# Attention stage of a gated block: row sums from TensorE to VectorE, W1 applied to the attended rows, norm of x on VectorE, bias on Pool

## The chip, the cores and the metric
One core of a Trainium2 chip runs the whole program. TensorE (PE) multiplies matrices from SBUF into PSUM; VectorE (DVE), ScalarE (ACT) and GpSimd (Pool) work on tiles of up to 128 partitions; SyncE (SP) issues most of the DMAs. The engines run at the same time and wait for one another only at semaphores; each takes its own instructions in the order in which they are written. The metric is the time of one execution in microseconds (us), less is better.

## The reference
x has 4 batches of 1024 rows of 256; the context has 154 rows for each batch. What matters, cut down:

```python
x = x + tanh(g_xattn[0]) * xattn(layernorm(x), ctx, w_sim, b_sim, W_qv, b_qv)
x = x + tanh(g_ffn[0]) * ffn(layernorm(x), w_gate, w_up, w_down)

def xattn(h, c, w_sim, b_sim, W_qv, b_qv):
    Sim = (h @ w1)[:, :, None] + (c @ w2)[:, None, :] + einsum('bid,bjd->bij', h * w3, c) + b_sim
    A = softmax(Sim, axis=2)
    hq = einsum('bij,bjd->bid', A, c)                    # attended
    Batt = softmax(max(Sim, axis=2), axis=1)
    hc = einsum('bi,bid->bd', Batt, h)                   # one row for each batch
    return concatenate([h, hq, h * hq, h * hc]) @ W_qv + b_qv
```

The feed-forward part quantizes activations and weights, with the largest values over whole tensors. W_qv has four blocks of 256 rows; W1 below is the second, which multiplies hq.

## The kernel before, in words
All x stays in SBUF (`xa`). The attention stage takes the rows in 16 pieces n of 256 rows, four to a batch b; s = n % 4. It is a pipeline by hand: one loop over m = 0 to 22, written out anew for each engine, in which step m does another operation for another piece. On PE, step m holds project(m - 7), turn_h(m) (transposes of the normed rows), score(m - 1), turn_a(m - 2) (transposes of the softmax), attend(m - 3) and turn_y(m - 8). In a step with m % 4 = 3 the project comes last ("late"), else first. The semaphores' counts order what the engines hand over; PSUM has one bank for each kind of result (`hT_bank`, `s_bank`, `a_bank`, `y_bank`, `hq_bank`, `m_bank`), and two for project.

A piece goes this way: VectorE takes mean and variance (`stats`, L955 to L962), Pool the power -0.5 (L363), VectorE the shift -mean x rstd (`row_shift`, L969), ScalarE the normed rows h (`norm_x`, L736). PE turns h, ScalarE copies hT (L744), PE scores (L454), VectorE adds the context's bias and takes the minimum (`scored`, L989), ScalarE the exponentials (L752), VectorE the reciprocal (L997), ScalarE scales (L761), PE turns, ScalarE copies aT (L768), PE attends (L474), VectorE multiplies the result in PSUM with hT (prT, L1005). Project (L491 to L499) sums three products into one bank: aT with `cw`, prT with W_qv's third block, hT with `we`. VectorE adds it to x (`residual`, L1013), takes the statistics of the second layer norm (L1017 to L1024), Pool the power (L367), VectorE writes y (L1030) and its maximum (L1057).

`cw` is the context times W1 plus the bias b_qv, once for each batch (`context_w`, L430, and `context_wv`, L978); since a softmax row sums to one, aT with cw gives attended x W1 with the bias. `we` holds W_qv's first block plus its fourth times hc. hc needs the softmax over a whole batch: `batch_max` and `batch_shift` take the extreme over 1024 rows, ScalarE the eight columns of weights eb (`batch_exp`, L801), PE the weighted row sums (`row_sum`, L537: eight matmuls, one for each 128 rows, M = 1), VectorE copies the row (`row_copy`, L1073), PE turns it to columns (`batch_cols`, L545), and `summary` (L1077 to L1083) writes we. For the first batch the eight row sums stand as a block in step 6; for the other three they stand between the matmuls of the project in the steps 10, 14 and 18. we(b) is needed by the late project of step 4b + 7.

Beside this run the preparations of the three feed-forward weights: scales on VectorE in m = 8, 12, 16 (L1097), two halves of `weight_q` on Pool (L380), int16 values on VectorE in m = 11, 15, 19 (L1117), a copy on ScalarE (L805), `weight_n` on Pool (L386).

## Time and profile before

| | |
|---|---|
| time, median of 3 runs | 500.15 us (500.15 to 500.7) |
| the profiled execution | 500.24 us, its span 498.0 us |
| PE busy | 467.1 us, 94% |
| VectorE busy | 347.6 us, 70% |
| ScalarE busy | 278.5 us, 56% |
| Pool busy | 42.8 us, 9% |
| mean granted PE clock | 0.983 |

The span runs from the first to the last instruction of the profile; the rest of the execution's time lies around it. The attention stage ends at about 222 us, where the quantized feed-forward part begins. Busy time of PE counts overlapping matmuls once, with modelled ends.

### The profile page before, as it was taken

How to read it: one execution, taken by the hardware profiler on the slowest of the kernel's cores; microseconds unless marked ns; L12 is line 12 of the kernel's file. 1: busy time of each engine (PE TensorE's matmuls, PEld its weight loads, DVE VectorE, ACT ScalarE, POOL GpSimd, SP SyncE). 2: the span in 40 equal slices, each digit the busy share in tenths (PEclk: the TensorE clock that was granted, in tenths of full speed). 3: DMA queues.
4: the chain of work that ended last, by engine and by line, in shares of the span. 5: the costliest groups of instructions: out<-in, count | busy, mean ns of one | idle time of the engine just before them, and what ended most of it. 6: DMA issues, size and time to landing. Idle time of an engine off the chain costs nothing.

```text
span 498.0 us, 6971 instructions
## 1 busy us (share of the span) xinstructions
PE 467.1 (94%) x2542; PEld 306.2 (61%) x2542; DVE 347.6 (70%) x648; ACT 278.5 (56%) x325; POOL 42.8 (9%) x51
## 2 busy tenths in 40 slices
PE   4899999998999979989999999999949999999997
PEld 3787885987488548754444444444414444588886
DVE  6464683687257754769443558999988888898874
ACT  3795241634151200528334379999977677888760
POOL 1111111242013110210000000000100000000000
PEclk9999999998999998999999999999969999999999
DMA  8920000200020020020000000000000000234432
GB/s 246 327 91 1 0 2 12 74 1 1 0 86 0 1 84 2 0 86 0 0 0 0 0 0 0 0 0 1 1 0 0 0 0 0 85 107 128 144 113 103
DMA packets 20671, 21.11 MB, mean 42 GB/s; under 512 B 826, under 2 KB 20393, under 8 KB 20649
## 3 DMA queue, kind: packets, MB, share of 16 engines
q1 hardware_dynamic: 20628, 20.82, 13.2%
q8 instruction: 13, 0.21, 0.2%
q14 instruction: 10, 0.07, 0.1%
q10 hardware_dynamic: 20, 0.00, 0.0%
HBM read 12.43 MB, written 8.39 MB: 42 GB/s over the span
## 4 chain that ended last, share of the span: by engine, by line
PE 56%; issue 17%; DVE 14%; ACT 10%; POOL 1%; DMA 1%; ACTq 0%; POOLq 0%; DVEq 0%
PE ps L672 11%; PE ps L647 10%; PE ps L652 5%; PE ps L495 4%; PE ps L491 4%; PE ps L474 4%; PE ps L499 4%; ACT ag L863 3%; PE ps L537 3%; ACT hid L870 3%; PE ps L454 3%; DVE hid L1279 2%; ACT gq L858 2%; PE ps L440 1%; PE ps L463 1%
## 5 line engine op out<-in xcount | busy, mean ns | idle before, releaser
L647 PE MATMUL ps<-xh,wuh 128*128 128x512 f16 x192 | 73.9, 385 | 9.3 <-DVE gq L1304 7.4
L647 PE MATMUL ps<-xh,wul 128*128 128x512 f16 x192 | 73.8, 384 | 0.0
L652 PE MATMUL ps<-xl,wuh 128*128 128x512 f16 x192 | 58.0, 384 | 0.0
L1251 DVE TENSOR_REDUCE cols<-hid x12 | 27.4, 2286 | 30.5 <-ACT hid L852 30.5
L852 ACT ACTIVATE hid<-ps 128x2048 f32 x12 | 22.5, 1875 | 34.5 <-PE ps L652 34.5
L647 PEld LDWEIGHTS ps<-xh,wuh 128*128 x192 | 19.0, 99 | 34.7 <-issue 11.2
L672 PE MATMUL ps<-wdh,oh 128*128 128x256 f16 x168 | 37.4, 273 | 0.0
L672 PE MATMUL ps<-wdl,oh 128*128 128x256 f16 x168 | 37.4, 273 | 0.0
L647 PE MATMUL ps<-xh,wgh 128*128 128x512 f16 x96 | 36.4, 379 | 0.7 <-DVE xh L1239 0.7
L647 PE MATMUL ps<-xh,wgl 128*128 128x512 f16 x96 | 36.4, 379 | 0.0
L491 PE MATMUL ps<-cw,aT 77*128 77x256 f32 x128 | 35.5, 392 | 0.9 <-ACT cols L801 0.9
L495 PE MATMUL ps<-wv,prT 128*128 128x256 f32 x128 | 35.9, 396 | 0.0
L744 ACT ACTIVATE hT<-ps 128x512 f32<-128x512 f32 x16 | 9.4, 590 | 46.5 <-PE ps L440 46.5
L499 PE MATMUL ps<-we,hT 128*128 128x256 f32 x128 | 33.5, 384 | 0.0
L652 PEld LDWEIGHTS ps<-xl,wuh 128*128 x192 | 19.0, 99 | 23.3 <-issue 1.1
L647 PEld LDWEIGHTS ps<-xh,wul 128*128 x192 | 19.0, 99 | 22.4 <-issue 1.1
L474 PE MATMUL ps<-aT,cx 77*128 77x256 f32 x128 | 30.5, 381 | 0.0
L1304 DVE TENSOR_TENSOR gq<-gq,ps 128x2048 bf16<-128x2048 int16 x11 | 25.2, 2287 | 6.1 <-ACT au L878 6.1
L1265 DVE TENSOR_REDUCE cols<-ps 128x1 f32<-128x2048 f32 x12 | 27.4, 2286 | 2.7 <-PE ps L652 2.7
L924 ACT ACTIVATE oq<-hid,cols 128x1536 int16 (+1 forms) x15 | 23.6, 1572 | 10.2 <-DVE ol L1349 10.2
L1310 DVE CUSTOM_DVE_ANT_0 hid<-pq,au 128x2048 f32<-128x2048 int16 x12 | 27.4, 2286 | 2.6 <-ACT pq L908 1.9
L495 PEld LDWEIGHTS ps<-wv,prT 128*128 128x128 f32 x128 | 23.8, 194 | 8.3 <-issue 5.2
(199 smaller groups left out, 945.9 us busy)
## 6 DMA issues: line engine op xcount, KB each, us to landing
x_scratch<-xa SPq DMA_DIRECT2D x4, 1024.0 KB, 4.4
xo<-x_scratch SPq DMA_DIRECT2D x16, 256.0 KB, 2.7
out_dram<-xo SPq DMA_DIRECT2D x15, 256.0 KB, 2.2
xa<-in_x SPq DMA_DIRECT2D x3, 1024.0 KB, 12.1
xa<-in_x SPq DMA_DIRECT2D x4, 256.0 KB, 4.7
wv<-in_L_xattn_W_qv SPq DMA_DIRECT2D x1, 1024.0 KB, 8.1
wr<-in_L_ffn_w_gate SPq DMA_DIRECT2D x1, 768.0 KB, 9.6
wr<-in_L_ffn_w_up SPq DMA_DIRECT2D x1, 768.0 KB, 11.0
```

Of the source, the lines that this page charges most:

```text
L474: mm = pe.matmul(hq_bank[:, d * PT:(d + 1) * PT], cx[b][0:JP, k, d * P:(d + 1) * P], aT[0:JP, par, k, q], start=k == 0, stop=k == 1)
L491: pe.matmul(o_, aT[0:JP, par, k, q], cw[0:JP, b % 3, k, :], start=k == 0, stop=False)
L495: pe.matmul(o_, prT[:, par, d, q], wv[:, 2 * KD + d, :], start=False, stop=False)
L499: mm = pe.matmul(o_, hT[:, par, d, q], we[:, par, d, :], start=False, stop=d == KD - 1)
L647: pe.matmul(ps[hf][:, q, :], w_[:, d, ds(k * P, P)], xh[:, d, n], start=d == 0 and w_ is wh, stop=False)
L652: mm = pe.matmul(ps[hf][:, q, :], wh[:, d, ds(k * P, P)], xl[:, d, n], start=False, stop=d == KD - 1)
L672: mm = pe.matmul(down_ps(par)[:, t], o_[:, par, k, q], w_[:, k, :], start=not low and k == 0 and w_ is wdh, stop=low and k == KF - 1)
L924: act.activation(oq[:, par], hid[:, :, ds(c * CD, CD)], ACT.Copy, scale=c_co).then_inc(oqa_rdy, 1)
L1251: dve.tensor_reduce(gmx[:, ds(k * 2 + hf, 1)], unit(hid, k, hf), AX.X, ALU.max, apply_absolute_value=True).then_inc(gm_done, 1)
L1265: dve.tensor_reduce(umx[:, u:u + 1], ps_half(u % 2), AX.X, ALU.max, apply_absolute_value=True).then_inc(half_free[u % 2], 1)
L1304: dve.tensor_tensor(g_.bitcast(BF16), g_, ps_half(hf), ALU.mult).then_inc(half_free[hf], 1)
L1310: dve.tensor_tensor_reduce(hid[:, k, hf * HALF:(hf + 1) * HALF], pq[hf][:], au[:, hf, :], 1.0, 0.0, ALU.mult, ALU.max, omx[:, u:u + 1]).th ...
```

## The change
- **Row sums.** The 32 matmuls go. VectorE forms the sum in place, in h's tile 0: h0 x eb0, then seven times h_t x eb_t + h0, each waiting for the one ahead (`hs_rdy`). Four links stand in s = 2 ahead of the reciprocal, four behind the product prT. Then h's tile 0 holds 128 rows of partial sums, and `batch_cols` sums them over the partitions by matmuls with a column of ones. `batch_cols` and `summary` move from s = 2 to s = 3, just ahead of the late project.
- **W1.** `context_w` and `cw` go. ScalarE copies the attended result from PSUM to `hqT` (behind its scaling), project multiplies hqT by W1, and prT is made from hqT and hT, both in SBUF. aT gets a ring of three.
- **Norm of x.** `row_shift` and ScalarE's norm_x go; VectorE does it in one tensor_scalar for each 128 rows ((x - mean) x rstd), for the piece m + 1, at the head of a step, in s = 3 behind summary.
- **Bias.** Pool adds tanh(g) x b_qv to x (`bias_x`), two pieces in each step with s = 0 or 3, once h of that piece is made; residual waits for it (`xb_rdy`).

The diff, cut to its core; of the two functions `attended`, the added one is ScalarE's.

```diff
+            def bias_x(n):
+                pool.wait_ge(h_rdy, n + 1)
+                if n == 0:
+                    pool.wait_ge(txb_rdy, 1)
+                x_ = xa[:, 2 * n:2 * n + 2, :]
+                pool.tensor_tensor(x_, x_, txb[:].unsqueeze(1).broadcast_to([P, 2, D]), ALU.add).then_inc(xb_rdy, 1)
...
                 if 1 <= m and m + 3 < N:
                     row_std(m + 3)
+                if s in (0, 3) and 4 <= m < N + 4:
+                    for n in range(2):
+                        bias_x(m - 4 + n if s == 0 else m - 5 + n)
...
-            def context_w(b):
...
             def attend(n):
                 pe.wait_ge(aT_rdy, n + 1)
-                ge(pe, pr_rdy, n)
+                ge(pe, hqT_rdy, n)
...
-                    for k in range(2):
-                        pe.matmul(o_, aT[0:JP, par, k, q], cw[0:JP, b % 3, k, :], start=k == 0, stop=False)
-                        if summed is not None:
-                            row_sum(summed, 4 * t + k)
+                    for d in range(KD):
+                        pe.matmul(o_, hqT[:, par, d, q], wv[:, KD + d, :], start=d == 0, stop=False)
                     for d in range(KD):
                         pe.matmul(o_, prT[:, par, d, q], wv[:, 2 * KD + d, :], start=False, stop=False)
-                        if summed is not None:
-                            row_sum(summed, 4 * t + 2 + d)
...
-            def row_sum(b, t):
-                mm = pe.matmul(m_bank[0:1, P:P + D], eb[:, t:t + 1], h[:, b % 2, t, :], start=(t == 0), stop=(t == TB - 1))
...
             def batch_cols(b):
-                pe.wait_ge(hrow_rdy, b + 1)
+                pe.wait_ge(hs_rdy, TB * (b + 1))
                 for d in range(KD):
-                    pe.matmul(m_bank[:, HC + d:HC + d + 1], hrow[0:1, d * P:(d + 1) * P], ones[0:1, 0:1], start=True, stop=True)
+                    pe.matmul(m_bank[:, HC + d:HC + d + 1], h[:, b % 2, 0, d * P:(d + 1) * P], ones[:, 0:1], start=True, stop=True)
...
+            def attended(n):
+                act.wait_ge(hq_ps, n + 1)
+                ge(act, f_ps, n - 2 * NP + 1)
+                act.activation(hqT[:, par, :, s * PT:(s + 1) * PT], hq_bank.rearrange("p (d n) -> p d n", d=KD),
+                               ACT.Copy).then_inc(hqT_rdy, 1)
...
+            def norm_x(n):
+                dve.wait_ge(rstd_rdy, n + 1)
+                ge(dve, hc_ps, b - 1)
+                for t in range(2 * s, 2 * s + 2):
+                    i_ = dve.tensor_scalar(h[:, par, t, :], xa[:, b * TB + t, :], mv[:, par, t, 0:1], rstd[:, c:c + 1],
+                                           ALU.subtract, ALU.mult)
...
             def attended(n):
-                dve.wait_ge(hq_ps, n + 1)
+                dve.wait_ge(hqT_rdy, n + 1)
...
+            def row_sum(b, tiles):
+                dve.wait_ge(eb_rdy, b + 1)
+                for t in tiles:
+                    ge(dve, hs_rdy, TB * b + t)
+                    if t == 0:
+                        i_ = dve.tensor_scalar(h[:, par, 0, :], h[:, par, 0, :], eb[:, 0:1], None, ALU.mult)
+                    else:
+                        i_ = dve.scalar_tensor_tensor(h[:, par, 0, :], h[:, par, t, :], eb[:, t:t + 1], h[:, par, 0, :],
+                                                      ALU.mult, ALU.add)
...
+                if s == 2 and 1 <= b <= B:
+                    row_sum(b - 1, range(0, 4))
                 if 1 <= m <= N:
                     normed(m - 1)
                 if 3 <= m <= N + 2:
                     attended(m - 3)
+                if s == 2 and 1 <= b <= B:
+                    row_sum(b - 1, range(4, TB))
+                if s == 3 and 1 <= b <= B:
+                    summary(b - 1)
+                if s == 3 and m + 1 < N:
+                    norm_x(m + 1)
                 if LAG <= m and late:
                     residual(m - LAG)
```

Two places in the engines' orders. First VectorE in step 10 (s = 2), before: the shift of piece 12, summary of the second batch, the unit of the first weight, y, reciprocal, product.

```order
L969 SCALAR_TENSOR_TENSOR cols<-cols 128x2
L1077 RECIPROCAL cols<-ps 128x1
L1079 TENSOR_SCALAR cols<-ps,cols 128x2
L1083 SCALAR_TENSOR_TENSOR we<-wv,cols 128x256 x2
L1107 TENSOR_REDUCE cols<-ps 128x1
L1109 TENSOR_SCALAR cols<-cols 128x1
L1110 RECIPROCAL cols<-cols 128x1
L1111 TENSOR_SCALAR cols<-cols 128x1
L1112 TENSOR_SCALAR wsc<-wsc,cols 128x48
L1030 TENSOR_SCALAR yb<-xa,cols 128x256 x2
L997 RECIPROCAL cols<-cols 128x2
L1005 TENSOR_TENSOR prT<-ps,hT 128x2x256
```

The same step of the changed kernel, from the unit's last instruction on (L1055 and L1057 are row_sum, L981 the product, L1034 the maximum of y).

```order
L1100 TENSOR_SCALAR wsc<-wsc,cols 128x48
L1006 TENSOR_SCALAR yb<-xa,cols 128x256 x2
L1055 TENSOR_SCALAR h<-h,cols 128x256
L1057 SCALAR_TENSOR_TENSOR h<-h,cols 128x256 x3
L973 RECIPROCAL cols<-cols 128x2
L981 TENSOR_TENSOR prT<-hqT,hT 128x2x256
L1057 SCALAR_TENSOR_TENSOR h<-h,cols 128x256 x4
L1034 TENSOR_REDUCE cols<-yb 128x1
```

The chain of eight has come in around reciprocal and product, and summary has left this step. Second, PE in step 11 (s = 3) before: attend, turn_y, context_bias and then the late project.

```order
L474 MATMUL ps<-aT,cx_84 128x256 x4
L510 MATMUL ps<-ident,yb 128x128 x4
L422 MATMUL ps<-cxT,w2b 128x154 x2
L491 MATMUL ps<-cw,aT 128x256 x2
L495 MATMUL ps<-wv,prT 128x256 x2
```

And in the changed kernel (L537 and L538 are batch_cols, L493 the product with W1).

```order
L477 MATMUL ps<-aT,cx_84 128x256 x4
L508 MATMUL ps<-ident,yb 128x128 x4
L435 MATMUL ps<-cxT,w2b 128x154 x2
L537 MATMUL ps<-ones,h 128x1 x2
L538 MATMUL ps<-cols,ones 128x1
L493 MATMUL ps<-wv,hqT 128x256 x2
L495 MATMUL ps<-wv,prT 128x256 x2
```

Batch_cols now stands directly ahead of the project that needs its result through VectorE's summary.

## Rows read from the trace of the kernel before

**Rows 1.** The page: busy us of an engine, share of the span, instructions.

```profile
PE 467.1 (94%) x2542; PEld 306.2 (61%) x2542; DVE 347.6 (70%) x648; ACT 278.5 (56%) x325; POOL 42.8 (9%) x51
```

**Rows 2.** Windows between late projects: length, busy of each engine (instructions), granted clock, DMA.

```profile
48.33:95.30 46.97, 46.97 (x251) 36.75 (x251) 29.42 (x103) 16.79 (x47) 8.04 (x10) 1.00 0.07 23
95.30:146.28 50.98, 48.13 (x243) 37.50 (x243) 31.08 (x96) 18.58 (x51) 10.78 (x10) 0.97 0.06 22
146.28:187.30 41.02, 37.11 (x179) 27.45 (x179) 26.17 (x64) 6.98 (x17) 8.41 (x7) 1.00 0.08 26
```

**Rows 3.** Waits of VectorE from 48.33 to 95.30: total us, times, longest.

```profile
DVE hrow L1073 <- PE ps L537: 7.7, 1, 7.7
DVE xa L1013 <- PE ps L499: 6.8, 3, 5.0
```

**Rows 4.** Chain of waits: start us, us, what; row sums alone, plain project, woven in.

```profile
36.81 3.54 PE ps L537 x16
...
48.33 0.86 PE ps L491 x4
...
52.65 0.86 PE ps L499 x4
...
74.46 0.52 PE ps L537 x2
74.98 0.63 PE ps L491 x2
...
83.91 1.06 PE ps L499 x4
```

**Rows 5.** Groups of instructions, 0 to 200 us: removed and replaced ones.

```profile
L495 PE MATMUL ps<-wv,prT 128*128 128x256 f32 x112 | 31.8, 398 | 0.0
L491 PE MATMUL ps<-cw,aT 77*128 77x256 f32 x112 | 31.4, 394 | 0.9 <-ACT cols L801 0.9
...
L430 PE MATMUL ps<-wv,cxT 128*77 128x256 f32 x32 | 7.7, 382 | 0.0
...
L978 DVE TENSOR_TENSOR cw<-ps,bqb 77x512 f32<-77x512 f32 x4 | 2.6, 653 | 0.0
...
L1073 DVE COPY hrow<-ps 1x256 f32<-1x256 f32 x4 | 1.6, 412 | 26.4 <-PE ps L537 26.4
```

**Rows 6.** By source line: durations min/median/max in ns, over the whole span.

```profile
L1083 DVE SCALAR_TENSOR_TENSOR we<-wv,cols x8: 473/484/1727, 44.0 to 183.3; 128x256 f32<-128x256 f32 x8
L1030 DVE TENSOR_SCALAR yb<-xa,cols x30: 402/409/1554, 56.4 to 212.5; 128x256 f32<-128x256 f32 x30
L1024 DVE TENSOR_SCALAR cols<-cols x15: 169/170/2506, 55.4 to 211.2; 128x2 f32<-128x2 f32 x15
```

**Rows 7.** Timeline in step 8: start us, us, engine, line, operation.

```profile
62.14 0.73 DVE L1030 TENSOR_SCALAR yb<-xa,cols 128x256 f32<-128x256 f32 x2
...
62.79 0.15 DVE L997 RECIPROCAL cols<-cols 128x2 f32<-128x2 f32 x1
...
62.98 0.74 ACT L761 ACTIVATE sc<-sc,cols 128x154 f32<-128x154 f32 x2 [0.31 <-DVE cols L997]
...
63.62 0.57 ACT L773 ACTIVATE yT<-ps 128x512 f32<-128x512 f32 x1
```

**Rows 8.** Timeline at the late project of step 15: residual's wait in brackets.

```profile
151.50 0.75 DVE L1013 SCALAR_TENSOR_TENSOR xa<-ps,cols,xa 128x512 f32<-128x512 f32 x1 [4.93 <-PE ps L499]
```

**Rows 9.** Timeline: Pool's weight work beside VectorE's small instructions.

```profile
94.17 1.48 POOL L380 TENSOR_TENSOR wr<-wr,wri 128x768 f32<-128x768 f32 x1
94.24 1.43 DVE L969 SCALAR_TENSOR_TENSOR cols<-cols 128x2 f32<-128x2 f32 x1 [0.28 <-POOL cols L363]
...
158.25 2.77 POOL L386 TENSOR_TENSOR wr<-wr,wsc 128x1536 f32<-128x1536 f32 x1 [3.96 <-ACT wr L805]
...
158.54 2.51 DVE L1024 TENSOR_SCALAR cols<-cols 128x2 f32<-128x2 f32 x1
```

**Rows 10.** PE's windows and the wait ahead: busy, granted clock (1.00 is 2.4 GHz).

```profile
186.78 0.72 PE L510 MATMUL ps<-ident,yb 128*128 128x128 f32 x4 [2.98 <-DVE yb L1030]
...
187.00:189.00 2.00, 2.00 (x9) 0.56 0.00 0
189.00:190.70 1.70, 1.70 (x6) 0.51 0.00 0
190.70:193.00 2.30, 2.30 (x12) 1.00 0.00 0
```

**Rows 11.** Timeline, end of the statistics in step 3.

```profile
27.69 0.17 DVE L962 TENSOR_SCALAR cols<-cols 128x2 f32<-128x2 f32 x1
```

More of the change, by code:

```diff
@@ L586, in _ @@
                 if LAG <= m and not late:
-                    project(m - LAG, b - 1 if s == 2 and 1 <= b <= B else None)
+                    project(m - LAG)
                 if s == 1 and 1 <= b <= B and LAG <= m:
@@ L597, in _ @@
                     score(m - 1)
-                if s == 2 and b == 1:
-                    pe.wait_ge(eb_rdy, b)
-                    for t in range(TB):
-                        row_sum(b - 1, t)
                 if 2 <= m <= N + 1:
@@ L814, in _ @@
             context_k(0)
-            norm_x(0)
             for m in range(N + LAG):
@@ L832, in _ @@
                     batch_exp(b - 1)
+                if 3 <= m <= N + 2:
+                    attended(m - 3)
                 if LAG < m:
@@ L1145, in _ @@
             stats(1)
-            row_shift(0)
+            norm_x(0)
             dve.wait_ge(bs_rdy, 1)
@@ L1194, in _ @@
                     attended(m - 3)
+                if s == 2 and 1 <= b <= B:
+                    row_sum(b - 1, range(4, TB))
+                if s == 3 and 1 <= b <= B:
+                    summary(b - 1)
+                if s == 3 and m + 1 < N:
+                    norm_x(m + 1)
                 if LAG <= m and late:
@@ L1197, in _ @@
                     norm_x1(m - LAG)
-                if s == 2 and b == 1:
-                    summary(b - 1)
                 if LAG <= m:
```

125 lines of the change are left out of this document (42 added, 83 removed).

## Prediction

> **What bounds the kernel now.** I read the busy shares first, then the chain of waits, then the windows of the stage that the change touches, and last the waits of VectorE there. TensorE (PE) is busy for 94% of the span, VectorE for 70% [rows 1]. The change lies in the attention stage, from the start to about 222 us; the feed-forward stage behind it keeps its instructions. In the chain nearly all of the stage from 31 us on is PE. I cut it at the starts of the four "late" projects (iterations m = 7, 11, 15, 19), at 48.33, 95.30, 146.28 and 187.3 us, and call the pieces A (0 to 48.33), B (46.97 us), C (50.98), D (41.0) and E (the rest). In B PE is busy all the time and VectorE for 29.42 us; in C 48.13 and 31.08, in D 37.11 and 26.17 [rows 2]. So PE sets the pace. VectorE's slack in B lies in two places: 7.7 us where it waits for the row sums and 6.8 us where it waits for a project's result [rows 3]. The question is whether PE's work goes faster than VectorE can follow.
>
> **What PE loses.** Eight row sums ran as a block in 3.54 us in the first batch. Woven into a project they cost more: that project runs from 74.46 to 84.97 us, 10.5 us, where a plain one takes 5.19 (48.33 to 53.52) [rows 4]. Four batches: 3.54 + 3 x 5.3 = 19.5 us. The attended x W1 through the context (L430, four blocks of 1.73 us in the chain) is 6.9 us more [rows 4, 5]. Project keeps its twelve matmuls: hqT with W1 (128 rows) stands where aT with cw (77 rows) stood, and wv,prT and cw,aT have the same mean, 398 and 394 ns [rows 5]. PE gives up 26.4 us in all. Batch_cols stays at three small matmuls.
>
> **What VectorE gains and loses**, for piece B. Removed: three shifts of 0.16 us (0.5), the sum into cw (0.65) and the copy of hrow (0.41) [rows 5]. Added: norm_x, two tensor_scalar of 256 elements; the same form, L1030, takes 0.65 us for the pair to its successor [rows 6, 7], so four times 0.65, one of them inside a gap that is there anyhow: 1.95. Added: the chain of eight; a scalar_tensor_tensor of 256 elements takes 473 ns at least, 484 in the median [rows 6], and each waits for the one ahead, about 0.03 us: 8 x 0.51 = 4.05 us. The product prT keeps its 512 elements and its price.
>
> **The waits that the change adds.** (1) The attended result is now copied out of PSUM by ScalarE, behind its scaling of the scores, and VectorE's product waits for that copy. At 62.79 us the reciprocal starts; ScalarE scales from 62.98, its next 512-element copy starts at 63.62 and takes 0.57 [rows 7]: ready at 64.2, where VectorE is ready at 62.94. That is 1.3 us in each of four iterations, 5.2 us; before, the product followed the reciprocal at 62.86. Behind it on VectorE stand the maximum of y, the next statistics and the next norm_x. (2) Summary moves from s = 2 to s = 3, straight ahead of the late project, which needs its `we`. So in s = 3 PE waits for VectorE's summary, and then VectorE waits for PE's project: this project's residual comes 5.25 us after its start. The gap was there before (4.93 us at 151.50 [rows 8]), but PE was working then and VectorE had time. Now both stand on one chain.
>
> **The sum for B**, along VectorE from one late project to the next: 29.4 busy, less 1.3 for a shift that a Pool instruction held at 94.24 us [rows 9] and less 1.55 for what is removed; plus 4.05 and 1.95 added; plus 1.2 of small gaps that stay (46.97 less 29.42 busy less the 16.4 of listed waits); plus 5.25 for the project, 5.2 for the hqT waits, 1.4 for exponentials that nothing covers in s = 1 and s = 3 (0.4 and 1.0), 0.8 for the standard deviation from Pool. That is 46.4 us. PE needs 46.97 - 5.3 - 1.7 = 40.0, so it waits some 6 us, most of it ahead of the late project. After such a wait it runs slower: in before it stood 3.0 us ahead of 186.78, and from 187 to 190.7 the granted clock is 0.51 to 0.56, the 1.2 GHz level; at 190.7 it is back at 2.4 GHz [rows 10]. 3.4 us of half speed cost 1.7 us, and they fall on the late project, on the chain. Pool's bias_x, 16 x two tiles of 256, takes about 1.05 us each (1.48 us for 768 elements, 2.78 for 1536 [rows 9]); Pool has time for it, but it can hold VectorE's instructions. I take 0.5 us a piece, between nothing and 2. B: 46.4 + 1.7 + 0.5 = 48.6, **+1.7**.
>
> **C**: 31.1 busy - 0.65 - 0.41 - 0.3 - 0.6 (a hold of summary that moves away) + 4.05 + 1.95 + 1.0 + 5.25 + 5.2 + 1.4 + 0.8 = 48.8, and 2.2 as above: 51.0, **0**. It held a PE wait and a low clock before too, which is why it comes out even. **D** (no norm_x, one hqT wait of 1.3): 26.2 - 1.25 (summary held by Pool in before, 2.13 instead of 0.88) - 0.4 + 4.05 + 0.9 + 5.25 + 1.3 + 1.4 + 0.7 (the last link, batch_cols and the way back, now open) = 38.2, and 2.2: 40.3, **-0.7**. **A**: the filling was paced by the round of PE, VectorE and ScalarE. Norm_x off ScalarE brings the first scores forward, some 0.7 us remain by m = 4. From the end of the statistics in m = 3 (27.9 us [rows 11]) to 48.33 were 20.5 us. Along VectorE now, m = 4: 0.65 + 0.37 + 0.5 + 0.4 + 1.0 + 0.15 + 1.3 + 0.6 + 1.15 less what overlaps, 5.65; m = 5, with the shift and batch_exp ahead of the copy, 5.75; m = 6, where the first four links cover the wait for the exponentials, 8.5; m = 7 to the end of summary 4.9. Together 24.8: **+3.6**. **E** is as before but for Pool's last bias_x ahead of the last weight scaling, **+0.3**.
>
> Together: 3.6 + 1.7 + 0 - 0.7 + 0.3 = 4.9. The profiled execution took 500.24 us with a span of 498.0, 0.09 above the median of three; 500.2 + 4.9 = **505.1 us**. What isn't measured: the chain's link (0.44 if the instructions overlapped, 0.71 at L1083's mean in the lines view, which holds come into: -2 or +7 over 32), the half clock (0 to 3.4 us in each of B, C, D against 1.7: -5 or +5), the holds by Pool (-2 to +6), and A (+-2).
>
> **A rule against a row.** L1083, with two inputs in SBUF, rose from 0.48 to 1.73 us, and L1024 from 0.17 to 2.51 while Pool's instruction ran from 158.25 to 161.0; it ended with it [rows 6, 9]. The Trainium skill (SBUF — State Buffer, section "SBUF: two separate sides") says that the two engines take a port pair as an exclusive lock for a whole instruction, and names VectorE instructions with two SBUF inputs among them. By that rule the product prT, whose input hq moves from PSUM to SBUF, and all links of the chain can be held by bias_x; the trace agrees for L1083 and shows nothing for prT. If every bias_x held VectorE for its whole length, the sum would be 16 x 1.05 = 16.8 us higher instead of 2.
>
> **The rivals.** *PE's relief counts (faster).* If the waits for the copy and for the late project fall away beside other work, each batch goes at PE's pace: 26.4 us less, 474 us; halfway between PE's 40.0 and VectorE's 46.4 in B (43.2, 3.8 us less) and alike in C and D, some 490. It needs VectorE below 40 us in B, where I find 46.4; for it speaks that VectorE idles 17.5 of 47 us in B today. Against it: 12 us of my 46.4 are waits that the order of the code forces. *About even.* The low clock doesn't come back at each batch (PE's wait is split) and the fill costs 1.5 less: 505.1 - 5.1 - 1.5 = 498.5, or with one of the two 500 to 503. *Pool and VectorE hold each other (slower still).* bias_x stands in s = 0 and s = 3, beside weight scales, norm_x and the quantized weights; with half its 16.8 us, and the links at 0.6 us, 505.1 + 6.4 + 2.9 = 514.4. It decides if holds on VectorE exceed some 3 us in total. The forecast itself ends on the slow side through the chain scores, copy, product, links, summary, late project: it decides at a VectorE path over 47 us in B.
>
> **How the numbers follow.** Forecast 502 to 509: 0.6. PE's relief, wholly or half: 0.15, below 498. Even, 498 to 502: 0.1. More holds, 509 to 516: 0.15. A measurement of this kernel tells some 0.2%, 1 us, from no change. Faster by over that: the relief and a third of the even case, 0.18. Within: 0.05. Slower: 0.77. The range leaves out most of the first rival and the far part of the last: 497 to 511.
>
> **What would show it.** In the profile of after: PE's busy time near 441 us and idle time of 4 to 6 us ahead of the late projects, ended by `we` of VectorE; granted clock near 0.5 there; VectorE waiting some 1.3 us for ScalarE's hqT ahead of each product, and 5 us for the project in s = 3; links of about 0.5 us. The late projects start near 52, 101, 152 and 192 us. Wrong would make it: PE without idle time in B (then the time falls), or products that find hqT ready, or a chain of 4 us that stands in VectorE's idle time.

## The result: 519.1 us against 500.15

The changed kernel takes **519.1 us** (median of 4 runs, 518.9 to 520.6) where the kernel before takes 500.15 (4 runs beside them, 499.4 to 500.7). The ratio is 1.0387, with a 95% interval of 1.0363 to 1.0411. The direction was forecast, the size was not: 505.1 was predicted, and 519.1 lies 14 us above it and 8 us above the range. Where the text below says "so many us by the ratios", the difference of two ratios to the kernel before is multiplied by 500.15 us, since each kernel was timed beside runs of the kernel before on its own chip.

First the page of the changed kernel: busy us of each engine, its share of the span, its instructions.

```profile
PE 459.2 (89%) x2446; PEld 314.4 (61%) x2446; DVE 374.7 (72%) x688; ACT 271.1 (52%) x309; POOL 63.5 (12%) x67
...
PEclk9989799679966986989999999999987999999999
...
PE 37%; DVE 23%; issue 21%; ACT 13%; POOL 4%; DMA 0%; ACTq 0%; POOLq 0%; DVEq 0%
```

Against [rows 1] PE has 96 rows fewer and is busy for only 7.9 us less, where 26.4 us were taken out: in the first half of the span the granted clock (third row, in tenths, 40 slices) drops again and again, and what is left runs longer. VectorE has 27 us more. Of the chain that ended last, PE now holds 37% and VectorE 23%.

The four late projects, where the prediction cut the stage, start at 53.08, 104.45, 157.93 and 204.55 us (52, 101, 152 and 192 were predicted). Windows between them, and from the last to the end: length, busy of PE, weight loads, VectorE, ScalarE and Pool (instructions), granted clock, DMA.

```profile
53.08:104.45 51.37, 45.11 (x226) 39.73 (x227) 35.26 (x115) 16.34 (x45) 13.54 (x14) 0.87 0.06 21
104.45:157.93 53.48, 44.65 (x219) 38.86 (x219) 37.31 (x105) 16.14 (x43) 15.31 (x13) 0.85 0.06 21
157.93:204.55 46.62, 36.81 (x162) 31.46 (x163) 33.53 (x70) 8.12 (x18) 13.45 (x11) 0.83 0.07 23
204.55:518.70 314.15, 296.74 (x1649) 173.68 (x1649) 235.46 (x260) 203.86 (x129) 10.85 (x12) 0.97 0.09 30
```

By [rows 2] the pieces are 4.4, 2.5 and 5.6 us longer (B, C, D), A is 4.75 longer and E, 314.15 against 310.7, 3.45. That is 20.7 us in all, 1.5 more than between the medians, since the profiled execution took 520.6 us. Predicted were +1.7, 0, -0.7, +3.6 and +0.3. Only A lies within its bound (+-2); B, C, D and E are off by 2.7, 2.5, 6.3 and 3.2 us.

The waits of B, the longest (total us, times, longest):

```profile
DVE xa L989 <- PE ps L497: 7.3, 1, 7.3
PE ps L493 <- DVE we L1071: 5.3, 1, 5.3
DVE prT L981 <- ACT hqT L747: 5.1, 4, 1.3
```

This is the picture that the prediction drew, with one number larger. PE waits 5.3 us for the new weights `we`, as foreseen (some 6). VectorE waits 1.28 us for ScalarE's copy in each iteration, four times (1.3 us, four times). And in s = 3 VectorE waits 7.3 us for the project's result. The residual was foreseen 5.25 us after the project's start and 1.7 more for the half clock, 6.95; it starts 7.8 us after it (60.89), since the half clock cost more than the prediction allowed. Three further rows by source line, over the whole span, give prices that had been assumed: links of 0.485 us, and 14 waits for `hqT` that add up to 18.4 us, as foreseen; bias_x, taken at 1.05 us, has 1.27.

```profile
L1057 DVE SCALAR_TENSOR_TENSOR h<-h,cols x28: 477/485/485, 41.4 to 201.1; 128x256 f32<-128x256 f32 x28
...
L394 POOL TENSOR_TENSOR xa<-xa,txb x16: 1259/1271/1320, 35.1 to 215.7; 128x512 f32<-128x512 f32 x16
```

```profile
L981 DVE TENSOR_TENSOR prT<-hqT,hT x16: 677/692/693, 24.8 to 198.9; 128x512 f32<-128x512 f32 x16
its engine sat idle before it (us, times) until:
  ACT hqT L747: 18.4, 14
```

### The profile page after: what moved, and what is told of

The parts are those of the page before. It is cut to its first block, busy times and chain, and to the rows that moved or that the text cites. A ratio compares the mean times of both kernels' runs of the same rounds, so it can differ in the third digit from the quotient of the medians.

```text
span 518.7 us, 6849 instructions
## 1 busy us (share of the span) xinstructions
PE 459.2 (89%) x2446; PEld 314.4 (61%) x2446; DVE 374.7 (72%) x688; ACT 271.1 (52%) x309; POOL 63.5 (12%) x67
## 4 chain that ended last, share of the span: by engine, by line
PE 37%; DVE 23%; issue 21%; ACT 13%; POOL 4%; DMA 0%; ACTq 0%; POOLq 0%; DVEq 0%
PE ps L654 11%; PE ps L629 10%; PE ps L634 5%; ACT ag L841 3%; ACT hid L848 3%; PE ps L493 3%; DVE yb L1006 3%; PE ps L495 2%; DVE h L1057 2%; PE ps L497 2%; DVE st L993 2%; DVE hid L1262 2%; DVE xa L989 2%; ACT gq L836 2%; ACT sc L724 2%
## 5 line engine op out<-in xcount | busy, mean ns | idle before, releaser
L493 PE MATMUL ps<-wv,hqT 128*128 128x256 f32 x128 | 38.4, 429 | 11.7 <-issue 6.4
L495 PE MATMUL ps<-wv,prT 128*128 128x256 f32 x128 | 36.3, 410 | 0.0
L493 PEld LDWEIGHTS ps<-wv,hqT 128*128 128x128 f32 x128 | 26.6, 218 | 15.6 <-issue 12.0
L477 PE MATMUL ps<-aT,cx 77*128 77x256 f32 x128 | 35.1, 423 | 0.2 <-ACT hqT L747 0.2
L497 PE MATMUL ps<-we,hT 128*128 128x256 f32 x128 | 34.9, 397 | 0.0
L989 DVE SCALAR_TENSOR_TENSOR xa<-ps,cols,xa 128x512 f32<-128x512 f32 x15 | 11.1, 738 | 31.5 <-PE ps L497 31.5
L784 ACT ACTIVATE wr<-wqi 128x1536 f32<-128x1536 int16 x3 | 4.5, 1484 | 52.0 <-DVE wqi L1105 52.0
L495 PEld LDWEIGHTS ps<-wv,prT 128*128 128x128 f32 x128 | 26.8, 210 | 4.4
```

The source lines that it names most:

```text
L477: mm = pe.matmul(hq_bank[:, d * PT:(d + 1) * PT], cx[b][0:JP, k, d * P:(d + 1) * P], aT[0:JP, n % 3, k, :], start=k == 0, stop=k == 1)
L493: pe.matmul(o_, hqT[:, par, d, q], wv[:, KD + d, :], start=d == 0, stop=False)
L495: pe.matmul(o_, prT[:, par, d, q], wv[:, 2 * KD + d, :], start=False, stop=False)
L497: mm = pe.matmul(o_, hT[:, par, d, q], we[:, par, d, :], start=False, stop=d == KD - 1)
L989: dve.scalar_tensor_tensor(x_, f_bank[n % 2].rearrange("p (t d) -> p t d", t=2), c_tx, x_, ALU.mult, ALU.add).then_inc(x1_rdy, 1)
```

## First round: one part of the change at a time

Two things in the trace were candidates for the missing 14 us. The first is Pool beside VectorE. Here is the place in step 15 where a residual has ended its statistics (timeline, all engines; start us, us, engine, line, operation):

```profile
168.07 0.17 DVE L1000 TENSOR_SCALAR cols<-cols 128x2 f32<-128x2 f32 x1
168.32 0.69 POOL L367 TENSOR_TENSOR cols<-cols 128x2 f32<-128x2 f32 x1 [22.58 <-DVE cols L1000]
...
168.97 2.54 POOL L394 TENSOR_TENSOR xa<-xa,txb 128x512 f32<-128x512 f32 x2
169.05 2.62 DVE L1006 TENSOR_SCALAR yb<-xa,cols 128x256 f32<-128x256 f32 x2 [0.81 <-POOL cols L367]
```

L1006 takes 0.73 us as a pair when nothing is beside it. Here it takes 2.62, as long as Pool's two bias_x: the first L1006 1.34 us beside a bias_x of 1.27, the second 1.35 beside one of 1.32. This is no accident of timing: both wait for the same thing. Pool computes the standard deviation of y (L367), VectorE needs it for L1006, and Pool goes on with bias_x at the very moment at which VectorE is released. Up to step 12 a row_std stands between the two in Pool's queue; behind it none does, and the pair meets each time, at 168.97, 178.39 and 214.49 us:

```profile
177.72 0.70 POOL L367 TENSOR_TENSOR cols<-cols 128x2 f32<-128x2 f32 x1
178.39 2.50 POOL L394 TENSOR_TENSOR xa<-xa,txb 128x512 f32<-128x512 f32 x2
...
213.83 0.69 POOL L367 TENSOR_TENSOR cols<-cols 128x2 f32<-128x2 f32 x1 [17.11 <-DVE cols L1000]
214.49 2.54 POOL L394 TENSOR_TENSOR xa<-xa,txb 128x512 f32<-128x512 f32 x2
```

Beside these VectorE has 2.62 us (for 0.73), 1.40 and 1.69 (for 0.29 and 0.73) and 2.62 again; beside the earlier bias_x it has 0.66 (for 0.17) at 69.02, 0.99 (for 0.29) at 77.41 and 131.76, and 0.36, 0.35 and 0.35 (for 0.19, 0.17 and 0.19) at 76.78, 121.17 and 131.14. That is 8.3 us more than the instructions' own time. All of them are tensor_scalar. Others ran beside a bias_x in their usual time: L989 with an input in PSUM (0.74 us at 67.18), L993 (0.42 for each half at 67.95), L1085 (1.75 at 75.00). The second candidate is the half clock at the late projects. And the waits for the copy, though foreseen, had to be tested: were they on the path as the prediction had it?

### Pool's bias left out

```diff
-                if s in (0, 3) and 4 <= m < N + 4:
-                    for n in range(2):
-                        bias_x(m - 4 + n if s == 0 else m - 5 + n)
...
-                dve.wait_ge(xb_rdy, n + 1)
```

> The changed kernel without Pool's bias_x and the waits for it; the bias b_qv of the residual is left out of what is computed. Theory (the holds that the trace of the changed kernel shows on VectorE beside bias_x, 0.99, 2.62, 1.40, 1.69, 1.88, 1.05, 1.88 and 2.62 us less the instructions' own 0.4 to 0.5, are on the path): some 8 us less than 519.1, 511. Rival, the prediction's 0.5 us a piece: 517. Rival, every bias_x (1.26 us, 16 of them) stands on the path: 499. Rival, the holds fall into waits that VectorE has anyway: 519.

(The list of holds in this text has three too many: the two of 1.88 and that of 1.05 us stand beside Pool's work on the weights, as a closer reading shows. Without them, with the second 0.99, the 0.66 and the three small ones, it is the list above, 8.3 us.)

Measured: 509.4 us, ratio 1.0183 (1.0162 to 1.0204). By the ratios bias_x costs **10.2 us**, five times what the prediction took (2.0) and more than its upper bound for it (+6 over that, 8). The windows between its late projects:

```profile
52.81:102.22 49.41, 42.92 (x226) 38.06 (x227) 33.96 (x115) 16.33 (x45) 8.60 (x10) 0.91 0.07 22
102.22:153.97 51.75, 44.46 (x218) 39.03 (x219) 35.91 (x105) 16.25 (x43) 10.57 (x9) 0.86 0.06 21
153.97:196.09 42.12, 34.23 (x162) 29.77 (x163) 29.55 (x70) 8.23 (x18) 8.46 (x7) 0.86 0.08 25
196.09:506.90 310.81, 295.29 (x1649) 172.12 (x1649) 233.59 (x260) 203.79 (x129) 8.32 (x10) 0.98 0.10 31
```

B and C are 2.0 and 1.7 us shorter than in the changed kernel, D 4.5 and E 3.3. VectorE's busy time in D falls from 33.53 to 29.55 us with the same 70 instructions: 4.0 us of its busy time there were holds, as the rows above have it (1.9 at 169 us, 2.1 at 178). In B and C VectorE's busy time falls by 1.3 and 1.4 us, again the list but for 0.4 in C. The late project of B is 0.7 us shorter besides (7.15 us from its start to the residual's, against 7.81), which makes up B's 2.0; of C's 1.7 us 0.6 stay open, since its late project is 0.3 longer without bias_x. In E the hold of 214 us has 1.9, and a further 1.9 is PE's wait for the last weights, which stand behind bias_x in Pool's queue: 3.02 us against 1.14 without it.

### The product first, then the copy

The product prT reads the attended result straight from PSUM again, and ScalarE's copy into hqT waits for it; project on PE waits for that copy instead of the product.

```diff
             def attended(n):          # ScalarE
-                act.wait_ge(hq_ps, n + 1)
+                act.wait_ge(pr_rdy, n + 1)
...
             def attended(n):          # VectorE
-                dve.wait_ge(hqT_rdy, n + 1)
+                dve.wait_ge(hq_ps, n + 1)
...
-                dve.tensor_tensor(prT[:, par, :, q], hqT[:, par, :, q], hT[:, par, :, q], ALU.mult)
+                dve.tensor_tensor(prT[:, par, :, q], hq_bank.rearrange("p (d n) -> p d n", d=KD), hT[:, par, :, q], ALU.mult)
```

> The changed kernel with the order of the two readers of the attended result turned round: VectorE multiplies prT straight from PSUM, and ScalarE copies hqT out afterwards. Theory (the 14 waits of 1.28 us, 18 us, stand on VectorE's path and VectorE's path sets the pace of the stage): 12 to 18 us less than 519.1, 501 to 507, since ScalarE has time for its copy until the next iteration. Rival (each wait only takes the place of one for the late project or for ScalarE's next result): 515 to 519. Rival (ScalarE's later copy makes its next results late): slower than 519.

Measured: 502.6 us, ratio 1.0046 (1.0025 to 1.0067), so **17.1 us** less than the changed kernel, of 18.4 us of waits. The product by source line:

```profile
L981 DVE TENSOR_TENSOR prT<-ps,hT x16: 664/680/692, 24.0 to 181.3; 128x512 f32<-128x512 f32 x16
its engine sat idle before it (us, times) until:
  PE ps L477: 0.6, 1
who waited for it (us, times):
  ACT hqT L747: 10.5, 3
```

The waits are gone, and reading PSUM instead of SBUF costs the product nothing (680 against 692 ns). ScalarE now waits three times for the product. That isn't free: PE waits 3.0 us for the later copy ahead of the second late project, and 6.1 us in D for the copy of yT, which stands behind that of hqT in ScalarE's queue. So nearly the whole wait for the copy lay on the path, as the prediction had it when it put 5.2 us a batch into its sum. It was not, as it read to be, a price of applying W1 to the attended result; it was the price of the order of two readers.

### Row sums back on PE

```diff
-                    project(m - LAG)
+                    project(m - LAG, b - 1 if s == 2 and 1 <= b <= B else None)
...
+                        if summed is not None:
+                            row_sum(summed, 4 * t + d)
...
-                if s == 2 and 1 <= b <= B:
-                    row_sum(b - 1, range(0, 4))        # VectorE
```

> The changed kernel with the 32 row sums back on PE, woven into project as before, the row copied by VectorE and summary back in s = 2; W1 through hqT, norm_x on VectorE and bias_x on Pool stay. Theory (VectorE sets the pace; it gives back 32 x 0.51 = 16 us and, since the new weights are ready one iteration ahead, the 5.2 us wait for the late project lies beside other work, while PE takes up 19.5 us that it has idle time for): 507 to 511. Rival (PE's relief is real and only the other three edits cost): 530 or more, with PE's row sums 12 to 19 us on the path. Rival (they cancel): 517 to 521.

Measured: 517.1 us, ratio 1.0347 (1.0325 to 1.0369), 2.0 us less by the ratios; the intervals of the two just overlap. The rival "they cancel" is right, or nearly. Why no 8 to 12 us came back is in the waits (40 to 245 us, total, times, longest):

```profile
PE ps L495 <- ACT cols L798: 11.7, 3, 5.3
```

L495 is the first matmul of the project with the woven sums, L798 the exponentials of the batch (0.9 us in all in the kernel before). VectorE, still late by the copies and by Pool, makes ScalarE's exponentials late, and the row sums on PE stand in front of a project that has nothing to do with them. The chain on VectorE needs no such wait on PE. Against this, the first three late projects now run at a granted clock of 1.00 (50.19 to 55.40, 99.62 to 104.80 and 152.40 to 157.60 us), which is worth some 7 us by the next round. So as the two kernels stand, the chain of eight costs about what PE's row sums, their wait and the clock come to together; none of the three is measured by itself.

### Norm_x back on ScalarE

The small shift goes back to VectorE with it; in s = 3 ScalarE's norm_x stands behind its copy of hqT (not shown).

```diff
-                if 3 < m and m + 1 < N and s < 3:      # VectorE
-                    norm_x(m + 1)
+                if m + 1 < N and s < 3:                # ScalarE
+                    norm_x(m + 1)
```

> The changed kernel with norm_x of x back on ScalarE (and the small shift back on VectorE). Theory (VectorE's 32 tiles of 0.4 us and the holds on them leave its path, ScalarE has room for them outside its way from the exponentials to the copies): 3 to 8 us less than 519.1, 511 to 516. Rival (ScalarE is as much on the round score, exponentials, scaling, copy, product as VectorE, and its norm_x stands ahead of the exponentials): 519 to 524.

Measured: 520.1 us, ratio 1.0401 (1.0378 to 1.0425), not to be told from the changed kernel. My theory, 3 to 8 us less, is wrong. The rival has the likelier sense: VectorE's 32 tensor_scalar leave its path, and ScalarE's stand ahead of its exponentials and copies. No run separates the two effects; that they are each of some size and cancel stays argued.

## Second round: the clock, the place of the bias, and the weave

### PE kept busy ahead of the late projects

Matmuls of ones with wv, which nobody reads, fill PE's idle time (11, 6, 5 and 3 ahead of the late projects, 6 and 8 ahead of two transposes).

```diff
                 if s == 0:
+                    for _ in range({0: 11, 4: 6, 8: 5, 12: 3}[n]):
+                        pe.matmul(f_bank[n % 2][:, 0:D], ones[:], wv[:, 0, :], start=True, stop=True)
                     pe.wait_ge(we_rdy, b + 1)
```

> The changed kernel with products that nobody reads put into PE's idle time: ahead of the late projects 11, 6, 5 and 3 matmuls of ones with wv (256 columns, f32, some 0.4 us each), and 6 and 8 ahead of two transposes of the scores that follow an idle time. Nothing of the computation is changed. Theory (the late projects of the changed kernel take 2.6, 2.45, 3.1 and 2.0 us more than 5.19 at a granted clock of 0.50 to 0.56, and stand on the chain summary, project, residual): 5 to 10 us less than 519.1, 509 to 514. Rival (the clock stays down all the same, or rises and VectorE is late for other reasons): 518 to 520. Rival (the extra matmuls overrun the idle time and push PE back): 520 to 525.

Measured: 512.5 us, ratio 1.0232 (1.0218 to 1.0247), **7.8 us** less by the ratios, though it adds work. The start of the late projects in the changed kernel, then here:

```profile
53.08:57.00 3.92, 3.92 (x9) 3.17 (x10) 0.50 (x2) 0.00 (x0) 0.00 (x0) 0.50 0.01 4
104.45:109.50 5.05, 5.05 (x13) 4.10 (x14) 0.55 (x2) 0.00 (x0) 0.00 (x0) 0.54 0.01 3
157.93:164.40 6.47, 6.47 (x17) 5.23 (x18) 0.00 (x0) 0.00 (x0) 0.00 (x0) 0.56 0.00 0
204.55:208.20 3.65, 3.65 (x9) 2.96 (x10) 0.00 (x0) 0.00 (x0) 0.00 (x0) 0.52 0.00 0
```

```profile
52.97:57.00 4.03, 4.03 (x19) 3.56 (x20) 0.59 (x2) 0.00 (x0) 0.00 (x0) 1.00 0.00 0
101.98:106.00 4.02, 4.02 (x19) 3.55 (x20) 0.59 (x2) 0.00 (x0) 0.00 (x0) 1.00 0.00 0
```

In the same 4 us PE has 9 rows at a clock of 0.50 and 19 at 1.00 (a matmul leaves two rows, a project 24), and the whole project stands between VectorE's summary and VectorE's residual. From their starts to those of the residuals behind them, the four late projects of the changed kernel take 7.8, 7.7, 8.3 and 7.2 us; in this run, at full clock, all four take 5.5. So the half clock (0.50, the level of 1.2 GHz) costs 2.3, 2.2, 2.8 and 1.7 us there, 9.1 together, and 7.8 of them came back. (The text above measures from 5.19 us, the length of a plain project alone, and gets somewhat more.) At the third, the low stretch alone is 6.5 us long, where [rows 10] had shown 3.7. The fourth isn't new: the kernel before has it too, as [rows 10] show, 7.0 us from 187.29 to the residual at 194.34, where its other three take 5.4.

### The bias where VectorE waits

On top of the product first: the four bias_x of a batch stand together in s = 3, behind norm_x, where VectorE waits for the late project, and ahead of y_std and row_std in Pool's queue.

```diff
+                if s == 3 and 4 <= m < N + 4:
+                    if m + 1 < N:
+                        pool.wait_ge(h_rdy, m + 2)
+                    else:
+                        pool.wait_ge(we_rdy, m // NP)
+                    for n in range(NP):
+                        bias_x(m - 7 + n)
                 if LAG <= m < L + LAG:
                     y_std(m - LAG)
```

> The run before it with prT first (502.6), and the four bias_x of a batch moved on Pool to one place: behind norm_x of s = 3, while VectorE waits for the late project's result (5 to 8 us, against 4 x 1.26). All is computed. Theory (the holds cost because Pool's bias_x follows y_std just when VectorE's next scaling is released; VectorE has nothing to run in the new place): 6 to 10 us less, 493 to 497, which is faster than the kernel before. Rival (the residual of the late project now waits for Pool): 500 to 505. Rival (the holds that cost are those of the quantized weights and not those of the bias): 501 to 503.

Measured: **492.3 us**, ratio 0.9816 (0.9777 to 0.9856): everything is computed, and it is faster than the kernel before. The move alone is worth 11.5 us by the ratios. Of the theory's 6 to 10 us that is somewhat more; the rivals are out. Pool's row and VectorE's at the third late project:

```profile
137.30 4.92 POOL L394 TENSOR_TENSOR xa<-xa,txb 128x512 f32<-128x512 f32 x4 [10.12 <-DVE we L1075]
```

```profile
136.34 0.88 DVE L1075 SCALAR_TENSOR_TENSOR we<-wv,cols 128x256 f32<-128x256 f32 x2
145.42 0.75 DVE L993 SCALAR_TENSOR_TENSOR xa<-ps,cols,xa 128x512 f32<-128x512 f32 x1 [8.20 <-PE ps L501]
```

The same four Pool instructions of 1.23 us run from 137.3 to 142.2, inside the 8.2 us in which VectorE has nothing to do.

### Both costs away

The two edits of the first round, the removal of bias_x and the product first, in one kernel:

```diff
-                act.wait_ge(hq_ps, n + 1)
+                act.wait_ge(pr_rdy, n + 1)
...
-                        bias_x(m - 4 + n if s == 0 else m - 5 + n)
```

> prT first and no bias_x at all (b_qv of the residual is left out of what is computed). Shows whether the two costs add up. Theory (they do: 16.5 and 9.7 us less than 519.1): 493. Rival (shorter waits in VectorE's path uncover PE, so that the second saving is smaller): 496 to 500.

Measured: 491.6 us, ratio 0.9811 (0.9797 to 0.9825). The copy (17.1 us) and the bias (10.2) add up: 1.0387 less 0.0341 less 0.0204 is 0.9842, measured 0.9811. With all four bias_x in VectorE's wait the time is the same as without them, within the intervals of some 2 us. So they are hidden there, and what they cost before was their place.

### The kernel before, row sums as a block

```diff
-                    project(m - LAG, b - 1 if s == 2 and 1 <= b <= B else None)
+                    project(m - LAG)
+                if s == 2 and 1 < b <= B:
+                    pe.wait_ge(eb_rdy, b)
+                    for t in range(TB):
+                        row_sum(b - 1, t)
```

> The kernel before with the row sums of the three later batches as a block behind the project of s = 2 instead of woven into it. Theory (what the prediction took: woven 5.3 us a batch, as a block 3.54): 3 x 1.8 = 5 us less than 500.15, 495. Rival (the weave hides the loads of the weights for the project, or the block delays the transposes that ScalarE waits for): 500 to 503.

Measured: 495.3 us, ratio 0.9876 (0.9855 to 0.9897). The prediction had worked out of [rows 4] that a woven batch of row sums costs 5.3 us and a block 3.54, so 5.3 us for three batches; 6.2 came by the ratios. A quarter of what the change took from PE was thus to be had on PE by itself.

## Third round: what is left, and a version that beats both

### The row sums on PE as a block, in the version of 492.3

```diff
+                if s == 2 and 1 < b <= B:              # PE, behind project
+                    pe.wait_ge(eb_rdy, b)
+                    for t in range(TB):
+                        row_sum(b - 1, t)
...
-                if s == 3 and 1 <= b <= B:             # VectorE
+                if s == 2 and 1 < b <= B:
                     summary(b - 1)
```

> The version of 492.3 us (prT first, the four bias_x together) with the row sums on PE as a block, hrow copied by VectorE, and summary in s = 2. Norm_x stays on VectorE. Theory (with VectorE relieved of its waits, both engines are near balance: PE takes up 4 x 3.5 = 14 us, of which the 13 us of idle time ahead of the late projects and their half clock, some 8 us, come back): 486 to 492. Rival (PE sets the pace once the waits are gone, so that each row sum costs what it takes): 498 to 506. It also tells what the chain of eight is worth by itself.

Measured: 491.8 us, ratio 0.9823 (0.9799 to 0.9847) against 0.9816. It lies at the edge of what my theory gave (486 to 492), but the plain reading is that nothing changes. It doesn't price the chain by itself, since two things move with it. PE has no wait directly ahead of the late projects any more, and the first two run at a clock of 1.00. And with summary in s = 2 the last two groups of bias_x wait for a `we` that is ready early: they meet the scaling of y again (1.29 and 1.35 us for 0.40 each, at 128.37 and at 175.21 us).

### Only W1 on the attended result

```diff
-                    for k in range(2):
-                        pe.matmul(o_, aT[0:JP, par, k, q], cw[0:JP, b % 3, k, :], start=k == 0, stop=False)
+                    for d in range(KD):
+                        pe.matmul(o_, hqT[:, par, d, q], wv[:, KD + d, :], start=d == 0, stop=False)
...
-                if s == 0 and 1 <= b < B:
-                    context_w(b)
```

> The kernel before with the row sums as a block (495.3), and on top only the edit of attended x W1: hqT copied out after prT is multiplied, W1 applied in project, no context_w, and the bias by Pool's four bias_x in s = 3. Row sums on PE, norm_x on ScalarE. Theory (PE loses four blocks of 1.73 us, 6.9 us, ScalarE gains 16 copies of 0.57 us off its path): 4 to 7 us less, 488 to 491. Rival (ScalarE's copy and Pool's bias_x cost as much): 494 to 497.

Measured: 494.9 us, ratio 0.9894 (0.9877 to 0.9911) against 0.9876 for the kernel with the block alone. In total the 6.9 us that PE loses with context_w bring nothing, as the rival had it. The traces show where they go. Cut at the late projects, this run is 1.2, 1.5, 0.9 and 1.5 us shorter than the block alone in A, B, C and E, 5.1 in all; D is 4.8 longer, 43.3 us (139.56 to 182.88) against 38.5. At its end, in this run and then in the one with the block alone:

```profile
176.24 5.02 POOL L395 TENSOR_TENSOR xa<-xa,txb 128x512 f32<-128x512 f32 x4 [0.36 <-DVE we L1093]
...
177.58 2.56 DVE L1037 TENSOR_SCALAR yb<-xa,cols 128x256 f32<-128x256 f32 x2
...
182.00 1.09 PE L512 MATMUL ps<-ident,yb 128*128 128x128 f32 x4 [7.02 <-ACT yT L782]
```

```profile
180.79 1.11 PE L504 MATMUL ps<-ident,yb 128*128 128x128 f32 x4 [2.94 <-DVE yb L1028]
```

PE is idle for 7.0 us instead of 2.9 ahead of the last transposes of y. Summary stands in s = 2 here, so `we` is ready early, Pool's four bias_x start at once and hold the scaling of y (2.56 us for 0.73); and ScalarE's copy of yT, for which PE waits, stands behind its copy of hqT, which waits 13.5 us for the product. The project that starts D, at a clock of 0.86, is 0.8 us longer besides. So W1 on the attended rows did bring some 5 us, and one place in D took them back; that a repair of it would keep them is not shown.

### Bias and product mended, and PE kept busy

The version of 492.3 with 6, 6, 3 and 3 matmuls that nobody reads ahead of the late projects, and 4 each ahead of two transposes.

```diff
                 if s == 0:
+                    for _ in range({0: 6, 4: 6, 8: 3, 12: 3}[n]):
+                        pe.matmul(f_bank[n % 2][:, 0:D], ones[:], wv[:, 0, :], start=True, stop=True)
                     pe.wait_ge(we_rdy, b + 1)
```

> The version of 492.3 us with products that nobody reads in PE's idle time ahead of the late projects (6, 6, 3 and 3) and ahead of two transposes of the scores (4 each). Nothing of the computation is changed. Theory (its late projects still take 2.0 to 2.6 us more than 5.2 at the lower clock, 8 us in four): 3 to 8 us less, 484 to 489. Rival (in this version PE is late by itself at two of the four places and the extra work pushes it back): 491 to 495.

Measured: **484.2 us**, ratio 0.9689 (0.9658 to 0.9720), the fastest of all, 3.1% under the kernel before. The windows between its late projects:

```profile
44.64:88.12 43.48, 43.48 (x247) 39.13 (x247) 33.74 (x115) 15.78 (x45) 13.56 (x14) 1.00 0.08 25
88.12:131.77 43.65, 41.88 (x233) 37.09 (x232) 35.58 (x105) 17.00 (x45) 15.52 (x13) 1.00 0.07 25
131.77:172.47 40.70, 34.61 (x168) 30.55 (x169) 29.53 (x70) 8.33 (x18) 14.50 (x12) 0.92 0.08 27
```

The clock is 1.00 in B and C, and B, 43.5 us, is 3.5 shorter than in the kernel before. This is about the case that the prediction called half of PE's relief (43.2 in B). In D PE still idles 6.1 us ahead of the last transposes of y, for the copy of yT behind that of hqT. The same filler was not tried in the kernel before, where one late project runs at the lower clock, so the 3.1% are not all the change's.

### The ledger without holds and without the half clock

```diff
-                        bias_x(m - 4 + n if s == 0 else m - 5 + n)
...
+                    for _ in range({0: 11, 4: 8, 8: 4, 12: 3}[n]):
+                        pe.matmul(f_bank[n % 2][:, 0:D], ones[:], wv[:, 0, :], start=True, stop=True)
```

> The changed kernel, its order of readers kept (ScalarE's copy first, with the 14 waits of 1.28 us), without bias_x (b_qv of the residual is left out of what is computed) and with products that nobody reads ahead of the late projects (11, 8, 4, 3) and of two transposes of the scores (5, 8). It leaves in the time only what the prediction had in its ledger besides Pool's holds and the half clock: 505.1 less 2.0 of holds and 5.1 of half clock, 498.0. Theory (the miss of 14 us consists of those two terms): 498 to 502, 8 to 11 us under the run without bias_x (509.4). Rival (the ledger's other terms, busy time and gaps, are short by several us): 503 to 508.

Measured: 506.9 us, ratio 1.0119 (1.0084 to 1.0153): 3.2 us under the run without bias_x, where 8 to 11 were expected; by the total the rival has it. The windows say more:

```profile
53.23:100.92 47.69, 45.31 (x252) 40.21 (x252) 33.99 (x115) 16.34 (x45) 8.63 (x10) 1.00 0.07 23
100.92:151.77 50.85, 46.23 (x243) 40.20 (x243) 35.96 (x105) 16.24 (x43) 10.58 (x9) 0.97 0.07 22
151.77:194.38 42.61, 36.19 (x168) 31.43 (x169) 29.55 (x70) 8.22 (x18) 8.47 (x7) 0.87 0.08 25
```

PE was kept at full clock through B only; ahead of the second and third late project it still waited 2.2 and 2.8 us for `we`, both ran 1.7 us long against the 5.5 of the filler's first run, and the fourth 1.3. The run without bias_x had 1.7, 2.5, 2.3 and 1.7 there, so the filler took 3.5 us off the late projects, and the time fell by 3.2: its expectation had counted on a full clock that it didn't get. The length of that last wait alone doesn't decide it: in the run of 512.5 us PE waited 3.0 us ahead of its second late project and stayed at 1.00 (its second window above). What does isn't settled. For B the comparison is clean: 47.7 us against the prediction's 46.4 without holds and half clock, so its ledger was 1.3 us short. With 1.7 us taken off C and D for the lower clock, C is 0.4 over the prediction's 48.8 and D 2.7 over its 38.2; A is 1.3 over and E 0.4 under. That is 5.3 us of the ledger in all. In D the waits show two places that the ledger had not priced:

```profile
186.00 0.65 PE L507 MATMUL ps<-ident,yb 128*128 128x128 f32 x4 [2.69 <-DVE yb L1008]
190.38 1.01 PE L536 MATMUL ps<-ones,h 128*128 128x1 f32 x4 [3.73 <-DVE h L1058]
```

PE waits 2.7 us for VectorE's scaled y and then 3.7 us for the last link of the chain.

## Why the prediction was wrong in size

**Right.** That VectorE, and not PE, would set the pace of the stage; that PE would wait some 5 us for `we` ahead of the late project (5.3) and VectorE behind it for the result; the wait of 1.3 us for ScalarE's copy in each iteration (1.28), and that it lies on the path (17.1 of 18.4 us, by the run with the product first); the link of 0.51 us (0.485, and a step of 0.51); the woven row sums at 5.3 us and the block at 3.54 (the kernel before with a block: 6.2 us less for 5.3). The first rival, PE's relief, fell as the prediction argued: with the row sums back on PE the changed kernel was only 2.0 us faster.

**Wrong: the holds by Pool, 2.0 us against 10.2.** This is the largest part of the miss, 8.2 of 14.0 us. The term was "0.5 us a piece, between nothing and 2", one piece being one of the windows; no working stands beside it, and no meeting of two instructions was looked up for it. In the last steps they don't meet by chance: Pool's bias_x follows y_std in its queue, and y_std is what releases VectorE's L1006. The order of Pool's queue was in the listing. The second thing that was missing is who stands behind bias_x on Pool: the last weight scaling was put down at 0.3 us and made 1.9. The question that was missing is what each engine does in the instant behind a semaphore that both have just passed. The rival "Pool and VectorE hold each other" named the effect and its point of decision (3 us of holds), and gave 514.4 us and a chance of 0.15.

**Wrong: the half clock.** The prediction took 1.7 us at each of three late projects, from the one stretch in [rows 10], 5.1 in all, and left the fourth as the kernel before has it. Measured, the first three take 2.3, 2.2 and 2.8 us longer, 7.3; the fourth 1.7, which was in the time before already. So by the lengths of the projects this is 2.2 us of the miss. Filling PE's idle time gives back 7.8 us, with the fourth among them, so about 1 by that run. The waits of PE ahead of the four were 5.3, 2.8, 2.2 and 1.5 us, that of [rows 10] 3.0; the length of the wait doesn't give that of the stretch. The bound of +5 that the prediction gave for it held.

**Wrong: the ledger of busy time and gaps.** What is left of the 14 us is 4 to 5; the last run, by its pieces, has 5.3. They are 1.3 in A, within its bound, 1.3 in B (47.7 against 46.4; 0.2 of it is the late project, 5.5 us to the residual at full clock for 5.25) and 2.7 in D. Of B's and A's the rest isn't settled. In D the prediction had counted a gain, since summary would no longer be held by Pool. The summary is not held; but Pool's quantized weights hold the scaling of y instead, which in the changed kernel stands ahead of the chain of eight, and PE's batch_cols waits for that. VectorE in D, in the changed kernel:

```profile
189.46 1.88 DVE L1006 TENSOR_SCALAR yb<-xa,cols 128x256 f32<-128x256 f32 x2 [0.62 <-POOL cols L367]
...
195.43 1.77 DVE L1006 TENSOR_SCALAR yb<-xa,cols 128x256 f32<-128x256 f32 x2
...
199.54 2.04 DVE L1057 SCALAR_TENSOR_TENSOR h<-h,cols 128x256 f32<-128x256 f32 x4
```

Two scalings of 1.88 and 1.77 us instead of 0.73, beside Pool's weight work of 1.5 us. There is no bias_x near them, and the run without bias_x has them too (1.88 and 1.77 at 181.0 and 186.96 us). A hold does not vanish when the instruction that it held moves away; it falls on what takes that place.

**The rule against the row.** The prediction weighed the Trainium skill's rule (SBUF — State Buffer, "SBUF: two separate sides") that VectorE and Pool take their shared ports for a whole instruction, and gave 16.8 us as its upper end. The runs agree with the rule where the two engines meet, in that L1006 lasts as long as Pool's pair beside it (2.62 and 2.54 us). They put the total at 10.2 us, since not every bias_x meets an instruction that it holds; and at nothing measurable where the bias_x stand in VectorE's wait. For the instructions that the prediction named, the product and the links, the changed kernel shows nothing: no bias_x ran beside one of them (693 and 485 ns at most). What was held were tensor_scalar.

**The range** (497 to 511) took the bounds of the terms one by one. Three terms were off, all to the slow side: the holds beyond their bound (8.2 us over, where +6 was given), the half clock within its own, and the busy time of B and D, which had been given none but for the link. That they went the same way is in part no chance, if a VectorE that is held makes PE wait longer and at a lower clock; in B the late project was 0.7 us longer with bias_x, in C 0.3 shorter, so this stays argued.

## What to carry to other kernels

Where two engines that can hold each other wait for the same event, look at what each issues next: that pair meets every time, and its cost is the length of the longer one less the held one's own time, not a share. Put such background work into a wait of the other engine that the chain forces anyway, and see that what starts it can't come early; here the move of sixteen instructions was worth 11.5 us. If a result in PSUM has two readers, let the one go first whose successor is due first (17 us here), and look at what stands behind the later one in its queue (6 to 7 us of PE in D). And work taken off an engine that sets the pace is worth something only up to where another takes over: the row sums as a block, 5.3 us less on PE, gave 6.2; the whole change, 26.4 us less on PE and more on VectorE, cost 19. With its waits mended and PE's idle stretches filled it came out 16 us faster than the kernel before, which the block alone makes 6 us faster.

## What the hardware showed that was not expected

VectorE's two small instructions of together 0.73 us were each held for one of Pool's, 1.34 and 1.35 us beside 1.27 and 1.32: between two instructions of Pool one of VectorE's got through. Even one of 2 columns was held so (L1000, 0.66 us for 0.17). The stretch at half clock was 3.7 to 6.5 us long behind waits of 1.5 to 5.3 us. And 39 matmuls of no use, of 0.45 us each (the first eleven took 5.00 us in the trace), made the kernel 7.8 us faster.
